# Four samples in one product of features, pairs put in place by DMA, loops unrolled

## The reference

```
e = stack([tbl_f[ids[:, f]] for f in range(26)], axis=1)
all_emb = concatenate([bottom[:, None, :], e], axis=1)        # 2048 x 27 x 128
gram = einsum('bfd,bgd->bfg', all_emb, all_emb)
h = concatenate([gram[:, triu_i, triu_j], bottom], axis=1)    # 351 + 128 = 479
h = maximum(h @ W_top1 + b_top1, 0)                           # 512
h = maximum(h @ W_top2 + b_top2, 0)                           # 256
y = h @ W_top3                                                # 1
```

## Time and profile before

| | |
|---|---|
| median of three runs | 460.55 us |
| profiled execution: span | 643.8 us |
| PE busy / weight loads | 395.4 / 296.7 us |
| DVE, ACT, POOL busy | 235.1, 310.4, 285.1 us |
| mean granted clock of PE | 0.759 |
| DMA | 50.39 MB, 78 GB/s |

### The profile page before, as it was taken

One profiled execution on the slowest core, in us unless ns is written; L12 is line 12 of the kernel. 1 busy time (PEld: TensorE's weight loads), 2 busy tenths in 40 slices (PEclk: granted clock), 3 DMA queues, 4 the chain that ended last, 5 costly groups with the idle time before them and its releaser, 6 DMA issues.

```text
span 643.8 us, 13317 instructions
## 1 busy us (share of the span) xinstructions
PE 395.4 (61%) x5324; PEld 296.7 (46%) x5324; DVE 235.1 (37%) x472; ACT 310.4 (48%) x470; POOL 285.1 (44%) x282
## 2 busy tenths in 40 slices
PE   2686572353578947625367894733536799467487
PEld 2464461232466835214256673412325578335375
DVE  3574560033286411030347822002135782202451
ACT  2484660056489512223559751412456983028832
POOL 7777357556003754664600573555550067250000
PEclk9798785565699987756568998955556899677689
DMA  5558442111224411111123441111121331010000
GB/s 157 165 184 230 168 139 58 38 40 44 91 98 134 144 41 43 45 47 36 49 81 109 152 126 29 51 42 43 41 68 57 132 114 50 25 42 6 8 4 0
DMA packets 21925, 50.39 MB, mean 78 GB/s; under 512 B 7288, under 2 KB 7320, under 8 KB 21744
## 3 DMA queue, kind: packets, MB, share of 16 engines
q1 hardware_dynamic: 12902, 30.96, 14.5%
q0 software_dynamic: 8832, 18.11, 10.6%
q10 hardware_dynamic: 138, 0.52, 0.2%
HBM read 49.00 MB, written 0.01 MB: 76 GB/s over the span
## 4 chain that ended last, share of the span: by engine, by line
PE 37%; issue 25%; another core or an unknown queue 13%; DMA 11%; ACT 9%; DVE 3%; SPq 0%; ACTq 0%; DVEq 0%
DMA table_raw<-in_tbl 11%; PE gram L442 11%; PE acc L421 5%; PE turned L403 5%; PE acc L422 4%; PE acc L449 4%; PE acc L451 4%; PE acc L450 3%; ACT pairs L559 3%; ACT table_hi L596 2%; DVE table_lo L716 2%; ACT features L577 1%; PE acc L509 1%; DVE onehot L732 1%
## 5 line engine op out<-in xcount | busy, mean ns | idle before, releaser
L368 POOL DMA_INDIRECT rows<-in_tbl,index x276 | 284.4, 1030 | 292.3 <-PE turned L403 157.0
L442 PE MATMUL gram<-features 128*26 128x26 f32 x4096 | 94.9, 213 | 151.8 <-issue 150.1
L421 PE MATMUL acc<-onehot,table_hi 125*128 125x512 f32 (+1 forms) x288 | 127.1, 441 | 50.2 <-DVE table_lo L716 22.7
L442 PEld LDWEIGHTS gram<-features 128*26 128x26 f32 x4096 | 70.7, 128 | 185.6 <-issue 183.3
L577 ACT COPY features<-turned 128x512 f32<-128x512 f32 (+2 forms) x80 | 82.2, 1062 | 139.4 <-remote 102.7
L422 PE MATMUL acc<-onehot,table_lo 125*128 125x512 f32 (+1 forms) x288 | 121.6, 422 | 0.0
L732 DVE TENSOR_SCALAR onehot<-wanted,row_number 125x512 fp32r<-125x512 int32 (+1 forms) x252 | 104.2, 475 | 33.7 <-PE acc L422 20.1
L557 DVE COPY aside<-gram 10x320 f32<-10x320 f32 x21 | 15.5, 737 | 234.6 <-remote 177.2
L421 PEld LDWEIGHTS acc<-onehot,table_hi 125*128 125x128 f32 x288 | 60.9, 211 | 71.8 <-issue 38.4
L559 ACT COPY pairs<-gram 18x128 f32<-18x128 f32 (+3 forms) x172 | 67.2, 390 | 1.5
L422 PEld LDWEIGHTS acc<-onehot,table_lo 125*128 125x128 f32 x288 | 60.9, 211 | 10.8
(11 more groups left out here) (40 smaller groups left out, 302.1 us busy)
## 6 DMA issues: line engine op xcount, KB each, us to landing
table_raw<-in_tbl SPq DMA_DIRECT2D x35, 500.0 KB
wanted<-in_onehot_ids SPq DMA_DIRECT2D x36, 256.0 KB
rows<-in_tbl,index POOLq DMA_INDIRECT x276
aside<-in_w SPq DMA_DIRECT2D x1, 1280.0 KB
bottom<-in_xT SPq DMA_DIRECT2D x4, 256.0 KB
h<-in_w SPq DMA_DIRECT2D x1, 512.0 KB
table_raw<-in_tbl ACTq DMA_DIRECT2D x1, 500.0 KB
pairs<-aside SPq DMA_DIRECT2D x16, 20.0 KB
```

The source lines that it names most:

```text
L368: pool.indirect_dma_start(out=rows[:, q % RING, f, :], out_offset=None, in_=gathered[f], in_offset=bass.IndirectOffsetOnAxis(ap=index[q // ...
L421: pe.matmul(to, table_hi[0:ROW_PARTS, i % TABLE_RING, c, :], of, start=(c == 0), stop=False)
L442: last = pe.matmul(gram[at:at + GRAM, q % 2, i // 4, 0:GRAM], features[:, q, i, 0:GRAM], features[:, q, i, 1:SLOTS], start=True, stop=True)
```

## The change

Four samples go through PE in one matmul: the stationary operand is 4 x 32 features (slots are padded from 27 to 32, zeros written once), the moving one 4 x 26, so the result is 128 x 104, of which only the four blocks on the diagonal are used. A tile is 32 such matmuls, in four chunks of eight groups; `gram` holds two chunks in four banks. The samples are permuted on the way in and the outputs on the way out.

The used blocks are copied out by `take_products`, quarter by quarter: of a chunk, 26 partitions x 208 values in one copy, four copies a chunk. It reads the 26 values of a sample next to each other and writes them to `products` at a distance of 128 values, 512 B. DVE takes three chunks of four, ACT one. When the whole block stands in `products`, SP moves it to `pairs` by 36 DMAs (nine for each quarter), now 3 columns wide, so layer 1 has 4 steps. DVE splits the pairs of a block in one piece, after the look-ups.

The ring of split tables has 3 places instead of 4. All loops are unrolled.

```diff
-TABLE_RING = 4
+TABLE_RING = 3
 TABLES_AHEAD = TABLE_RING - 1
+PACK = 4
+RUN = P // PACK
+WIDE = PACK * GRAM
+BANK = 512
+BANK_GROUPS = 4
+CHUNK_GROUPS = 2 * BANK_GROUPS
-PAIR_TILES = 4
+PAIR_TILES = 3
+TRIPLES = [(24, 26), (21, 24), (18, 20), (15, 18), (12, 14), (9, 11), (6, 8), (3, 5), (0, 2)]
...
-        features = sb("features", [P, BLOCK_TILES, P, SLOTS])
+        features = sb("features", [P, BLOCK_TILES, P, QUADRANT])
-        pairs = sb("pairs", [P, 2, PAIR_TILES, P])
-        aside = sb("aside", [P, 2, ASIDE, P])
+        products = sb("products", [P, GRAM, P])
+        pairs = sb("pairs", [P, PAIR_TILES, BLOCK])
-        gram = psum("gram", [P, 2, P // 4, QUADRANT])
+        gram = psum("gram", [P, 2, 2, BANK])
...
-                for i in range(P):
-                    at = QUADRANT * (i % 4)
-                    last = pe.matmul(gram[at:at + GRAM, q % 2, i // 4, 0:GRAM],
-                                     features[:, q, i, 0:GRAM], features[:, q, i, 1:SLOTS], start=True, stop=True)
+                at_least(pe, act_products, chunks_taken(ACT_CHUNKS, n - 1))
+                at_least(pe, dve_products, chunks_taken(DVE_CHUNKS, n - 1))
+                for i in range(CHUNK_GROUPS):
+                    t = (j % TILE_CHUNKS) * CHUNK_GROUPS + i
+                    at = (i % BANK_GROUPS) * WIDE
+                    last = pe.matmul(gram[:, n % 2, i // BANK_GROUPS, at:at + WIDE],
+                                     features[:, q, t * PACK:(t + 1) * PACK, :].rearrange("d s f -> d (s f)"),
+                                     features[:, q, t * PACK:(t + 1) * PACK, 1:SLOTS], start=True, stop=True)
...
-                copy(to(aside, 0, ASIDE, ASIDE), of(ASIDE, 1, ASIDE))
-                for j in range(4):
-                    last = copy(to(pairs, QUADRANT * j, COLUMN_ROWS[j], PAIR_TILES),
-                                of(COLUMN_ROWS[j], COLUMNS_FROM[j], PAIR_TILES))
+            for s in range(PACK):
+                at = slice(QUADRANT * s, QUADRANT * s + GRAM)
+                of = gram[at, n % 2, :, 0:BANK_GROUPS * WIDE].rearrange("f k (t n) -> f k t n", n=WIDE)
+                last = copy(products[at, :, first:first + CHUNK_GROUPS].rearrange("f g (k t) -> f k t g", k=2),
+                            of[:, :, :, s * GRAM:(s + 1) * GRAM])
...
-                for c, columns, n in ASIDE_MOVES:
-                    sp.dma_start(pairs[row:row + n, q % 2, 0:columns, :],
-                                 aside[0:n, q % 2, c - 1:c - 1 + columns, :]).then_inc(aside_landed[q % 2], 16)
+                for g, n in TRIPLES:
+                    k = 1 if g == 0 else 0
+                    sp.dma_start(pairs[row:row + n, k:PAIR_TILES, s * P:(s + 1) * P],
+                                 products[QUADRANT * s:QUADRANT * s + n, g + k - 1:g + PAIR_TILES - 1, :]
+                                 ).then_inc(pairs_landed, 16)
...
+                move_pairs(b, 0)
+                if more:
+                    load_wanted(b + 1, 3)
+                    load_raw(b + 1, 4)
+                move_pairs(b, 1)
+                if more:
+                    load_wanted(b + 1, 4)
+                    load_raw(b + 1, 5)
+                move_pairs(b, 2)
+                if more:
+                    load_wanted(b + 1, 5)
+                    load_raw(b + 1, 6)
+                    load_index(b + 1, 1)
+                move_pairs(b, 3)
+                if more:
+                    load_wanted(b + 1, 6)
+                    load_raw(b + 1, 7)
+                    load_wanted(b + 1, 7)
...
+                for j in range(BLOCK_CHUNKS):
+                    if j % TILE_CHUNKS in DVE_CHUNKS:
+                        products_out(b, j)
+                    if more and 8 <= j:
+                        onehot_chunk(b + 1, 0, j - 8)
+                    if more and j in (14, 15):
+                        table_low_part(b + 1, j - 14)
+                if more:
+                    onehots(b + 1)
+                    split_pairs(b)
+                    split_h1(b)
```

More of the change, by code:

```diff
@@ L35 @@
 BLOCKS = BATCH // (P * BLOCK_TILES)
-TILES = BLOCKS * BLOCK_TILES
 BLOCK = P * BLOCK_TILES
@@ L243, in at_least, with group_number, chunks_taken @@
+        def group_number(b, q, g):
+            return (b * BLOCK_TILES + q) * GROUPS + g
+        def chunks_taken(chunks, n):
+            return sum(j % TILE_CHUNKS in chunks for j in range(n))
         def at_least(eng, semaphore, count):
-            if not (isinstance(count, int) and count <= 0):
+            if count > 0:
                 eng.wait_ge(semaphore, count)
-        def gated(eng, name, semaphore, count):
-            at_least(eng, semaphore, count)
-            if not isinstance(count, int):
-                eng.sem_inc(gate[name], 1)
@@ L459, in layer1, with turn @@
                     at = slice(m * P, (m + 1) * P)
-                    return product(acc[:, (fill + m) % 2, samples], w1_hi[:, k, at], w1_lo[:, k, at], x_hi, x_lo,
-                                   step == 0, step == K1 - 1 and samples.stop == BLOCK)
-                ahead = 0 if turn else 2
+                    return product(acc[:, (fill + m) % 2, :], w1_hi[:, k, at], w1_lo[:, k, at], x_hi, x_lo,
+                                   step == 0, step == K1 - 1)
+                def turn(step):
+                    if more and step in TURN_STEPS:
+                        transpose_group(b + 1, 1, TURN_STEPS.index(step))
@@ L479, in mlp @@
[L479 to L483 removed]
+                pe.wait_ge(pairs_split, b + 1)
+                for m in range(M1):
+                    if m >= ahead:
+                        pe.wait_ge(acc_out, fill + m - 1)
+                        layer1(m, 0)
+                    for step in range(1, K1):
```

570 lines of the change are left out of this document (229 added, 341 removed).

## The result

The changed kernel takes **529.7 us** (median of four, 526.65 to 532.76) where the kernel before takes 463.05 in the same session (four runs, 460.23 to 465.61): ratio 1.143, 95% interval 1.135 to 1.151. The forecast was 492. The direction and the largest term (SP's moves) were right, the size was not: 67 us more, not 32.

A forecast was written before the change was run, and what follows sets the result against it. It took issue of PE's product records to bound the product stretch, 34.5 us a block. 460.5 + 2 (products, copies) - 3 (layer 1) + 24 (end) + 10.5 (look-ups) - 2 (small edits) = 492 us; range 456 to 542.

The forecast's parts named there:

- rival D: Product stretch: the profile's starving is partly real, G nearer 44 us, so the change is faster, 438 us; chance 0.13.
- G: Length of one block's product stretch in the kernel before, without the profiler; taken as 34.5 us.
- neither sign of being wrong: Stated signs the forecast is wrong: the end grows by less than 15 us, or G was never near 35.
- Products: PE's matmuls of four samples: 87 ns a record, 28.3 us a block with turns, no longer limited by issue.
- so the load hides: PE's products: loading 128 stationary columns instead of 26 adds no time, since turns with such a load run near their columns alone.
- Copies: Copying products out: 533 ns on DVE, 640 on ACT; with PE 35 us a block, +2 us in all.
- B: Rival on copying out: strided writes bind, 0.85 us a copy, +12 us a block, 538 us; chance 0.15.
- C: Rival on PE's products: low clock of 1.2 GHz, 54.4 us a block, 570 us; chance 0.05.
- Layers: Layer 1 with 4 steps instead of 5, less a later split of pairs: -1.1 us in each of three blocks.
- The end: Last product to the end: 36 uncovered moves at 0.73 us on SP's queue, 56.7 us against 32.8, +24 us.
- E: Rival on SP's moves: the profiler also inflates SP's issuing, 465 us, no measurable change; chance 0.17.
- The look-ups: Table loads behind groups of nine moves on SP: some 45 us instead of 41.7, +3.5 in three blocks, +10.5 us.

The follow-up runs named there:

- narrow_weights: Changed kernel with only the first sample's 26 of 128 stationary columns used in each product, moving operand still 104 columns: 518.28 us.
- two_queues: Changed kernel, but in the last block ACT issues 18 of the 36 moves while SP issues the other 18: 515.09 us.
- one_move_again: Changed kernel with 1 of the 9 moves of each quarter, 4 a block instead of 36: 470.57 us.
- six_only: Changed kernel with the 36 moves of the first three blocks in sixes between the look-ups' loads, nothing else: 502.02 us.
- spread_moves: Changed kernel with, in blocks 0 to 2, three moves between two loads and 21 behind the last: 529.37 us.
- three_queues: Changed kernel with moves in sixes, copies in runs of 8, earlier table splits, last block's moves on SP, ACT and POOL, pairs split by quarters: 466.93 us.
- narrow_moving: Changed kernel with only the first 26 of 104 moving columns of each product computed, stationary operand still 128 columns: 607.41 us.

## Why the prediction was wrong

**Ground.** The earlier trace rows were read as the profiler's doing. More likely they are what one chip does, and rival D, which needs G over 43, is out. G = 34.5 us was close to the four unstarved stretches, 35.1, 31.5, 34.2 and 33.3 (mean 33.5, between it and the forecast's other reading of 32.3), but by luck: the 34 came from 15 us put outside the span, where the run of that trace has 1.8 (458.67 against 456.9), and from 62 us of look-ups and layers, which are 67 (three times 5.4 short, 16 us). The two errors nearly cancel. Two of the forecast's signs say nothing for the same reason. The profiled span did fall, by 119 us, but because the span before was no picture of a usual chip. And neither sign of being wrong came (the end grew by 27, G was near 35), though the forecast was off: neither of them watched the look-ups.

**Products: a term mis-sized, for the wrong engine.** The forecast had 87 ns a record and DVE as the pace, +0.5 us a block. PE is the pace, with 110 ns a record: 23 ns x 256 = 5.9 us a block more on PE. The step "so the load hides" failed: 14 of the 23 ns go with a narrow stationary operand (`narrow_weights`), the other 9 stay open. 28 us of records, 4 of turns and 1.8 of output layer make 34 of the 36.6. The earlier trace rows held the warning: four turns with the same load took 0.59 us, 147 ns each, where 0.83 ns a column gives 107. The forecast called that near.

**Copies: the price was right, their place in the stretch was not.** 516 ns measured, 533 forecast, 506 on ACT instead of 640. B needed 0.6 us or more and is out; DVE waits 52.9 us for products. But cheaper copies still gave 10 us, so they are not free. C is out too: the clock was 1.00 in block 1's products.

**Layers: the direction was right**, -2.3 a block against -1.1, since the split (956 and 1758 ns, forecast 2.8 us together) stood almost wholly under PE's last look-up.

**The end: right**, 27 against 24. The bulk was 36 issues in 29.85 us (forecast 26.3), shown by `two_queues` and `one_move_again`. E, cheap issuing, is out.

**The look-ups: this step failed**, +10 to +13 us a block against +3.5. The forecast followed SP's queue from the last copy: table 7's load at 32 us, last one-hot at 44.7. Measured from the last copy's end (130.1 us) the load is at 36.4 and the last one-hot ends at 50.1, 5.4 later: 2.5 because the moves began so late, behind a table load that itself waited for a low part (L594); 1.9 because nine moves and the loads take 8.4 to 8.7 us a table, not 7.7; 1 in the tail. Another 4.2 lie ahead of that copy, which DVE starts only after a one-hot and a low part (126.75), and 1.9 behind, PE's last matmuls: 56.2 from product to look-up. These 6.1 us were left out by the way of counting: the forecast's 44.7 ran from the last copy to the last one-hot, and it was set against 41.7 that ran from the last product to the last look-up. The stretch of before was 45, not the 41.7 read from the starved trace, which takes 3.3 back. `six_only` showed that the order of nine moves was worth 28 us, and `spread_moves` that another order can be worth nothing: a forecast that asks only when each load is issued, and never adds up SP's queue with its waits, can't tell the two apart.

So of the 38 us missed, 24 were in the look-ups, 12 in the products, 3 in the end and 1 in the start, less 4 in the layers; the rest lies in which runs are compared.

## What to carry to other kernels

Before packing a stage, ask what leaving most of it out would save (here 14 us for three quarters): that is about the ceiling, and the regrouping that the packing needs comes on top. Take the price of issuing a small transfer from a row of the same shape (here 0.75 to 0.95 us each, from 39 KB down to 2 KB); multiply their number by that price, place it on one in-order queue, and then ask who waits behind them and whether the queue itself ever waits. When two stretches are compared, count both between the same two events. When a stage's waits move to another engine without changing the time, count the queue's total work before blaming the traffic.

## What the runs showed of the hardware

- A move inside SBUF of 2 to 26 partitions in three dimensions costs its issuer 0.83 us from start to start (`x36` in 29.85 us), on SP and on ACT alike (`x12` in 10.0 and 10.2); the median record is 784 ns. Of one quarter's nine in the last block, the first and largest (39 KB) took 0.95 us and the later ones 0.76 to 0.88, the last (2 KB) among them. On POOL the median record of such a move was 588 ns (`three_queues`). A contiguous read back from DRAM in two dimensions took 322 ns, a 500 KB table 0.28 to 0.35 us.

```profile
L246 SPq DMA_DIRECT2D pairs<-products x144: 681/784/1267, 132.6 to 496.8; - x144
L224 SPq DMA_DIRECT2D pairs<-scratch x32: 253/322/939, 140.9 to 458.8; - x32
```

- The Trainium skill ("SBUF — State Buffer", section "Door 1", the note on cachelines) says that accesses that each touch a new 16-byte line pay. The copies agree on both engines: the same 208 values take 370 ns on DVE in runs of 8 and 516 with 512 B between values, on ACT 323 and 506, although the order of the reads from PSUM changed with it. DVE's copy of slot 0, 108 B apart in 688 ns, shows no such price, so the rule does not hold for every copy here.
- An FP32 matmul with 128 stationary columns took 110 ns a record with 104 columns streamed, at a granted clock of 1.00, and 204 ns with 26 streamed, at 0.50; by the clock the second would be 102 ns at 1.00, an estimate.
- In `narrow_moving` (26 columns streamed for each 128 loaded) PE was busy for all of the 15 us from 100 to 115 us by its records, and the granted clock there was 0.50 (1.2 GHz). In the changed kernel (104 streamed) it was 1.00 (2.4 GHz) in block 1's products, with PE busy for 35.05 of 36.60 us.
- On one chip the four edited kernels that ran there, all with gathers beside products, show waits of up to 15 to 20 us on DVE without a releaser, and the kernel before took 653.56 us for 463. What on that chip does it stays open.
